# Causal mask of transposed attention scores: VectorE's minimum on the exponentials instead of identity products

## What is computed

```python
x = x + _layernorm(_L0_attn_ref(_layernorm(x), W_attn, b_attn, W_proj, b_proj))

def _L0_attn_ref(x, W_attn, b_attn, W_proj, b_proj):   # 16 heads of 16 columns
    q, k, v = split(x @ W_attn + b_attn)                # q and k then get the rotary factors
    att = einsum('bhqd,bhkd->bhqk', q, k) / sqrt(hd)
    att = where(tril, att, -inf)                        # causal
    y = einsum('bhqk,bhkd->bhqd', softmax(att), v)
    return y.reshape(B, T, C) @ W_proj + b_proj
```

## Time and profile before

| | |
|---|---|
| three runs | 3014.14, 3021.38, 3021.91 us |
| median | 3021.38 us |
| the profiled execution's own time | 3020.04 us |
| its span in the trace | 3018.3 us |
| busy share of the span | TensorE 85%, VectorE 54%, ScalarE 40%, GpSimd 30% |

### The profile page before, as it was taken

The page is one execution under the profiler, slowest core; times in us unless marked ns, Lnnn a source line. Parts: engine busy times, 40 slices in busy tenths (PEclk is TensorE's granted clock), DMA queues, the critical chain, the costliest instruction groups (busy, mean ns, idle before and its releaser), DMA issues. The chain is left out here.

```text
span 3018.3 us, 40610 instructions
## 1 busy us (share of the span) xinstructions
PE 2563.3 (85%) x14316; PEld 1528.3 (51%) x14316; DVE 1633.8 (54%) x4637; ACT 1206.3 (40%) x1994; POOL 910.8 (30%) x1442
## 2 busy tenths in 40 slices
PE   3799999999999999995158888947899999999997
PEld 2244444444545444442137777734566666656664
DVE  2667676767677675772743444342444443443443
ACT  1266666666566666564122232202322322322221
POOL 6040524426160716134012111011324233243142
PEclk9699999999999999998577887968999999999999
DMA  2442250605251524301401111121111021021010
GB/s 96 120 127 72 87 154 35 197 32 170 61 179 51 160 81 141 86 17 56 151 4 54 34 50 52 46 56 48 51 35 44 31 69 43 29 71 43 15 43 28
DMA packets 156117, 220.25 MB, mean 73 GB/s; under 512 B 18591, under 2 KB 122987, under 8 KB 149676
## 3 DMA queue, kind: packets, MB, share of 16 engines
q1 hardware_dynamic: 151820, 213.65, 23.0%
q0 software_dynamic: 4096, 4.01, 0.5%
HBM read 113.75 MB, written 103.88 MB: 72 GB/s over the span
## 5 line engine op out<-in xcount | busy, mean ns | idle before, releaser
L1009 ACT ACTIVATE pt<-ps 128x1024 f32<-128x1024 f32 (+3 forms) x768 | 599.8, 811 | 308.3 <-PE ps L924 210.3
L835 DVE CUSTOM_DVE_ANT_0 masked<-ps,mask_q 128x128 bf16<-128x128 f32 (+3 forms) x1024 | 473.4, 485 | 246.1 <-PE ps L902 243.9
L902 PE MATMUL ps<-sk,sq 96*128 96x512 bf16 (+3 forms) x1536 | 427.7, 337 | 66.5 <-DMA sk<-scratch_stacks 28.9
L921 PE MATMUL ps<-sq,sk 99*128 99x512 bf16 (+3 forms) x1536 | 398.7, 329 | 13.6 <-DMA sq<-scratch_nm_parts 11.5
L839 DVE TENSOR_REDUCE mx<-ps 128x1 f32<-128x512 f32 x512 | 351.7, 687 | 91.0 <-PE ps L902 90.5
L940 PE MATMUL ps<-pt,val 128*32 128x512 f32 (+3 forms) x3072 | 328.1, 499 | 3.5 <-ACT yt L1017 3.5
L902 PEld LDWEIGHTS ps<-sk,sq 96*128 96x128 bf16 x1536 | 132.6, 97 | 385.6 <-issue 104.1
L2086 PE MATMUL ps<-w_fc,eyb 128*128 128x256 f32 x1024 | 229.3, 381 | 14.6 <-ACT eyb L2147 7.8
L921 PEld LDWEIGHTS ps<-sq,sk 99*128 99x128 bf16 x1536 | 147.4, 98 | 161.0 <-ACT pt L1009 59.1
L2074 PE MATMUL ps<-eht,w_fc 128*128 128x512 f32 x512 | 223.2, 594 | 1.5 <-ACT eht L2137 1.4
L2086 PEld LDWEIGHTS ps<-w_fc,eyb 128*128 128x128 f32 x1024 | 191.4, 190 | 49.3 <-ACT eyb L2147 16.1
(11 more groups left out here) (329 smaller groups left out, 4295.6 us busy)
## 6 DMA issues: line engine op xcount, KB each, us to landing
scratch_stacks<-part SPq DMA_DIRECT2D x32, 768.0 KB, 3.7
sq<-scratch_stacks SPq DMA_DIRECT2D x32, 768.0 KB, 8.9
sk<-scratch_stacks SPq DMA_DIRECT2D x32, 768.0 KB, 11.4
scratch_stacks<-part SPq DMA_DIRECT2D x32, 512.0 KB, 4.6
scratch_x<-xr SPq DMA_DIRECT2D x16, 1024.0 KB, 7.7
x<-in_L_attn_x SPq DMA_DIRECT2D x8, 1024.0 KB, 14.4
scratch_stacks<-part SPq DMA_DIRECT2D x32, 256.0 KB, 4.9
xr<-in_L_attn_x SPq DMA_DIRECT2D x8, 1024.0 KB, 6.3
```

The source lines that it names most:

```text
L835: nc.vector.tensor_tensor_reduce(mem["masked"][:, slot, 0:n], ps[:, RING[slot], 0:n], mem["mask_q"][:, BANK - n:BANK], 1.0, -3e38, ALU.add ...
L902: nc.tensor.matmul(ps[:, bank, 0:n], sq[0:ROWS, h, i * P:(i + 1) * P], sk[0:ROWS, h, half * BANK:half * BANK + n], start=True, stop=True)\
L921: last = nc.tensor.matmul(ps[:, bank, 0:n], sk[0:ROWS_M, h, j * P:(j + 1) * P], sq[0:ROWS_M, h, q0:q0 + n], start=True, stop=not diag)
L1009: nc.scalar.activation(pt[:, u % 3, 2 * pair:2 * pair + 2, 0:n], ps[:, bank:bank + 2, 0:n], ACT.Exp, scale=SCALE).then_inc(e["exp_done"], 1)
```

## The change

The identity products and their tiles (`ident16`, `mask_kq`, `zeros16`) go. Instead a tile `cap` holds 3e38 where a key may be seen and 0 where not, and for each unit on the diagonal VectorE takes the minimum of the exponentials' first 128 columns and `cap`, for four heads in one instruction ("clip", 128x512 f32, two SBUF operands). In the list of steps the clip of unit t-1 stands in turn t between part 0 and part 1 of the steps beside (exp 0, part 0, exp 1, clip, part 1, av, y_out, part 2). The value products come two units behind instead of one (`AV_LAG = 2`) and wait for the clips up to their unit; "t1" moves one turn later.

```diff
+UNBOUND = 3e38
@@ setup, GpSimd
-                nc.gpsimd.affine_select(out=w["mask_kq"][:, :], in_=w["zeros16"][:, :], compare_op=ALU.is_ge,
-                                        fill=NEG, base=0, pattern=[[1, P]], channel_multiplier=-1)
+                nc.gpsimd.memset(mem["cap"][:, :], UNBOUND).then_inc(capped, 1)
+                g.wait_ge(capped, 1)
+                nc.gpsimd.affine_select(out=mem["cap"][:, :], in_=mem["cap"][:, :], compare_op=ALU.is_ge,
+                                        fill=0.0, base=0, pattern=[[1, P]], channel_multiplier=-1)
@@ setup, VectorE
-                nc.vector.memset(mem["mask_q"][:, 0:BANK - P], 0.0)
-                nc.vector.memset(w["zeros16"][:, :], 0.0).then_inc(zeroed, 1)
+                nc.vector.memset(mem["mask_q"][:, 0:BANK - P], 0.0).then_inc(zeroed, 1)
...
-                nc.vector.tensor_copy(w["ident16"][:, :], w["ident"][:, :]).then_inc(turned, 1)
@@ order of the steps
+AV_LAG = 2
+def on_diagonal(g):
+    half, j, q0, n = EU[g]
+    return q0 == j * P
+def clips_until(t):
+    whole, rest = divmod(t, len(EU))
+    return whole * sum(on_diagonal(g) for g in range(len(EU))) + sum(on_diagonal(g) for g in range(rest))
...
-            put(behind + 1 + i // 2, ("t1", b, i))
+            put(behind + 2 + i // 2, ("t1", b, i))
...
         if t < turn * B:
-            for pair in range(2):
-                order += [("exp", t // turn, *divmod(t % turn, n_eu), pair)] + cut[pair]
+            order += [("exp", t // turn, *divmod(t % turn, n_eu), 0)] + cut[0]
+            order += [("exp", t // turn, *divmod(t % turn, n_eu), 1)]
         else:
-            order += cut[0] + cut[1]
+            order += cut[0]
         if 0 < t <= turn * B:
             b, (s, g) = (t - 1) // turn, divmod((t - 1) % turn, n_eu)
+            order += [("clip", b, s, g)] if on_diagonal(g) else []
+        order += cut[1]
+        if AV_LAG <= t < turn * B + AV_LAG:
+            b, (s, g) = (t - AV_LAG) // turn, divmod((t - AV_LAG) % turn, n_eu)
             order.append(("av", b, s, g))
@@ VectorE
+                if kind == "clip":
+                    s, g = a
+                    u = turn * b + s * n_eu + g
+                    v.wait_ge(e["exp_done"], 2 * u + 2)
+                    nc.vector.tensor_tensor(pt[:, u % 3, :, 0:P], pt[:, u % 3, :, 0:P],
+                                            spread(mem["cap"][:, :], 1, HS), ALU.min).then_inc(e["clipped"], 1)
@@ TensorE, exp and av
-                        diag = q0 == j * P
                         last = nc.tensor.matmul(ps[:, bank, 0:n], sk[0:ROWS_M, h, j * P:(j + 1) * P],
-                                                sq[0:ROWS_M, h, q0:q0 + n], start=True, stop=not diag)
-                        if diag:
-                            last = nc.tensor.matmul(ps[:, bank, 0:P], w["ident16"][:, :], w["mask_kq"][:, :],
-                                                    start=False, stop=True)
+                                                sq[0:ROWS_M, h, q0:q0 + n], start=True, stop=True)
...
                     pe.wait_ge(e["exp_done"], 2 * t + 2)
+                    if on_diagonal(g):
+                        pe.wait_ge(e["clipped"], clips_until(t + 1))
```

More of the change, by code:

```diff
@@ L119, in setup_attention @@
         masked = m.sem("masked")
+        capped = m.sem("capped")
         zeroed = m.sem("zeroed")
@@ L217, in _ @@
                     nc.vector.tensor_copy(w["wqkv"][:, k, 2 * C:3 * C], wqkv_raw[:, k, 2 * C:3 * C])
-                    nc.vector.tensor_scalar(bvrep[:, k, :], ones[:, :], bv[:, k:k + 1], None, ALU.mult)
-                nc.vector.tensor_copy(w["ident16"][:, :], w["ident"][:, :]).then_inc(turned, 1)
+                    last = nc.vector.tensor_scalar(bvrep[:, k, :], ones[:, :], bv[:, k:k + 1], None, ALU.mult)
+                last.then_inc(turned, 1)
                 v.wait_ge(cols, 1)
@@ L401 @@
 TABLES = {
-    "ident": ([P, P], F32), "ident16": ([P, P], BF16), "mask_kq": ([P, P], BF16),
-    "zeros16": ([P, P], BF16), "zeros32": ([P, P], F32), "mask_f32": ([P, P], F32),
+    "ident": ([P, P], F32), "zeros32": ([P, P], F32), "mask_f32": ([P, P], F32),
     "bdmask": ([P, HC, S1], F32), "mhalf": ([P, NT], F32),
@@ L646, in attention_loop @@
             "junk": m.sb("junk", [P, NT, C], BF16),
-            "mask_q": m.sb("mask_q", [P, BANK]), "masked": m.sb("masked", [P, len(RING), BANK], BF16),
+            "mask_q": m.sb("mask_q", [P, BANK]), "cap": m.sb("cap", [P, P]), "masked": m.sb("masked", [P, len(RING), BANK], BF16),
         }
         names = """x_in x_stat head_step x_rstd x_ready
-            parts_step nm_ready nm_step nmp_ready nm_out s_full exp_done av_done yt_ready xr_in a_stat tail_step a_rstd a_norm x1_ready x1_stat x1_rstd xn1_ready
+            parts_step nm_ready nm_step nmp_ready nm_out s_full exp_done clipped av_done yt_ready xr_in a_stat tail_step a_rstd a_norm x1_ready x1_stat x1_rstd xn1_ready
             x1_stored scored keep_step kept xn2_ready x2_ready stored""".split()
@@ L829, in _ @@
                     slot, uses = bank_use(step)
-                if kind == "max":
+                if kind == "clip":
[4 more added lines that the diff above has]
+                                            spread(mem["cap"][:, :], 1, HS), ALU.min).then_inc(e["clipped"], 1)
+                elif kind == "max":
                     s, n_unit = a
```

## The result

The changed kernel takes 3077.34 us, the median of four runs (3073.4 to 3084.2), against 3018.18 before: a ratio of 1.0199 [1.0173, 1.0224], +59 us where +19 was forecast. The forecast's time was 3039 us, and the range ended at 3072: the measured time lies above it. Its profiled execution has a span of 3073.8 us; a body in the middle of the loop (mean of five) takes 170.5 us instead of 163.5.

What follows compares the result with a forecast made beforehand. VectorE's fullness was to decide in some stretches, TensorE's pace elsewhere. Terms 2.88 - 1.29 + 0.80 gave +2.4 us a body, +19 over 8 bodies on 3020.0: 3039 us; range 3003 to 3072.

Steps and rivals of the forecast that it cites:

- A: Stretches into and through set 0: +1.33 us a body, from turns 10, 11 and 2, 3; turns 0, 1 shorter by 0.48.
- B: Set 1's stretches: turns 10, 11 +0.46 us, turns 0 to 3 with room -0.96, together -0.50 us a body.
- C: Set 2's stretches: turns 10, 11 +0.91 us, turns 0 to 3 -0.96, together -0.05 us a body.
- D: Set 3's stretches: turns 10, 11 +0.94 us, 0, 1 +1.09, 2 to 4 +1.51, together +3.54 us a body.
- Turn by turn: Sum over a body's stretches, each the greater of VectorE's time with clips and old length less products: +2.88 us a body.
- VectorE has 8 us of room: Set 2, where GpSimd is busy 18.88 of 20.24 us: VectorE's room covers its exclusion by GpSimd, so nothing is added.
- GpSimd's 0.8: Set 3's turns 0 to 4: five clips wait for GpSimd operations that exclude VectorE, +0.8 us a body.
- Identity products: 1024 products hold 61 us of TensorE, 0.24 us a turn; time saved in turns 10 and 11 is waited away.
- Value products one unit later: Wide ones leave turns 1 and 5, lightening them where TensorE sets the pace: -1.29 us a body.
- Faster: the clips are hidden: Rival: clips fit VectorE's gaps around TensorE's score pairs; 2968 us, or 3003 if only set 3 pays; chance 0.22.
- No difference: the clip is cheap: Rival: a clip costs 0.45 us instead of 0.60, +0.1 us a body, 3021 us; chance 0.16.
- Dearer: GpSimd and VectorE shut each other out: Rival: clips in set 3 and turns 10, 11 of sets 1, 2 wait whole GpSimd operations; 3072 us; chance 0.15.

Runs made afterwards that it cites:

- clip_half: Changed kernel with clips of 64 instead of 128 columns a head, the rest of the mask left out: 3037.18 us, 1.0057 of the kernel before.
- place_by_set: Changed kernel with the clips of set 1's turns 1 to 4 and set 2's turns 2 and 3 moved to their turn's end: 3067.77 us, 1.0152.
- clip_last: Changed kernel with every clip moved to the end of its turn, behind all the maxima beside it: 3135.71 us, 1.0379 of the kernel before.
- reduce_instead: Changed kernel with each clip replaced by a maximum over the same 512 elements with one SBUF operand, mask left out: 3075.86 us, 1.0182.
- no_mask: Changed kernel without clips, and without identity products, so no causal mask on the transposed scores: 2992.66 us, 0.9914 of the kernel before.
- clip_unit8: Changed kernel with VectorE's clip for unit 8 alone and identity products for the other units: 3010.95 us, 0.9966 of the kernel before.
- lag_alone: Changed kernel's order of steps alone, with identity products kept and no clips: 3017.75 us, 0.9995 of the kernel before.
- mix_a: Changed kernel with GpSimd's select for unit 8 of all sets and units 0 to 3 except in set 2, identity products elsewhere: 3010.61 us, 0.9971.
- clip_early: Changed kernel with value products one unit behind and t1 where it was before the change: 3202.69 us, 1.0606 of the kernel before.
- both_masks: Changed kernel with identity products kept beside the clips on the diagonal: 3097.44 us, 1.0262 of the kernel before.

## Why the prediction was wrong in size

The direction was right, and so were the mechanism in the stretches where VectorE was counted as the fuller and the price of a clip in VectorE's queue. The time was 38 us short of the measured one, the change 40 us: the clips cost 86 us where 60 were forecast, the products gave 25 instead of 31, the later value products 2 instead of 10. By sets, against the forecast, a body lost 0.6 us more in A, 2.7 in B and 2.2 in C, and 0.8 less in D: the miss lies in B and C.

**The step that failed** is the rule of "Turn by turn": "A stretch's new length is the greater of its VectorE time plus 0.60 a clip, and its old length less 0.24 a masked turn", with "turns 0 to 3 have room" and the clip of turn 4 "hidden in the same way". It compares two sums of busy time over a stretch, as if work could be moved within it. VectorE works through a list, and a clip ahead of a maximum can delay that maximum, and TensorE behind it, even where VectorE idles later in the same turn. The table shows 5.3 us a body, 42 us in all, in stretches to which the rule gave 0; clip_half shows that the cost goes with the length. What lies behind it differs by set:

- B, 2.18 us: shown. place_by_set and clip_last give back 1.8 of it by moving the clips behind the maxima.
- C, 2.17 us: shown for some 0.6, the exclusion of GpSimd (reduce_instead); 0.46 of it is the clip of turn 4, whose cost clip_last leaves as it was. The prediction gave GpSimd nothing here, since "VectorE has 8 us of room": the same step. Of the rest, clip_last gives back the 0.42 of turn 3. Some 1.1 us in turn 0 stay open: that they are the clip's place is read from the list alone, and clip_last doesn't shorten that turn.
- A, turns 0 and 1, 1.08 us: not the place. The forecast took 6.10 us as the length without clips (5.67 with the later value products); the order alone made it 4.59, and so VectorE decides there too.

For turn 4 the prediction said "where that cover fails each costs up to 0.60"; it cost 0.57 in B, 0.56 in C (seen in turn 5) and nothing in A.

**The other terms of the sum:**

- Clips in the full stretches: forecast +6.7 a body and +0.8 for GpSimd in D, measured +5.9; D's clips last 0.67 to 0.74 us, so GpSimd's 0.8 isn't there. D's total agrees, +3.54 over turns 10 to 4, measured 5.72 + 6.97 + 9.24 - 5.08 - 6.05 - 7.30 = +3.50, but in part by luck: turns 10, 11, 0 and 1 cost 0.5 us less than forecast, and turns 2 to 4 cost 0.4 more, about what the clock costs there (last section). Turns 10 and 11 were dear in the forecast (+3.2 in four sets) and cost 1.95.
- All clips: forecast 60 us (7.5 x 8), measured 86: 42 us more where 0 was given, 13 us less where they were priced (1.6 x 8), by the profile's bodies.
- Identity products: 3.84 a body, 31 us; measured 3.8 a body and 25 us in the runs. Turns 4 to 9 gave 1.43 (forecast 1.44 for turns 8 and 9). That the sum agrees is luck: turns 0 to 4 gave 1.7 (forecast 2.40), and turns 10 and 11, where the saving should be "waited away", 0.65.
- Value products one unit later: -1.29 a body, measured -0.36. A gave -0.77 (forecast -0.86; turns 0 and 1 lost 2.0 us and turns 4 to 9 gained 1.1, more than the moved products hold, as "t1" moved too), B -0.31 (-0.43), but C lost 0.61 and D 0.11 where lighter and heavier turns were to cancel: turns 10 and 11 grew by 0.9 in the four sets, D's turns 2 to 4 by 0.43, and the turns that the wide products left gave little in C and D.
- The price of a clip, 0.60 us in the queue, was right (0.59 from the clip to the next maximum), as were 0 for the value products' wait (0.2 us in all). The prediction gave 0 also for VectorE's wait for the exponentials; the clips' group has 52.3 us of idle time before it, but in all bodies except the last it lies at the clip of turn 9 (1.4 us in B and C, 1.0 in D), and turn 9 is as long as without clips (3.60 us in B and C).

**The rivals.** "Faster: the clips are hidden" falls with no_mask and clip_half. It named the right gaps, "around TensorE's score pairs", but a clip uses one only if it stands in front of it; the clip of turn 9 costs nothing, and clip_unit8, which has it alone, is faster. "No difference: the clip is cheap" falls with 685 ns a clip. "Dearer: GpSimd and VectorE shut each other out" came nearest in time (3072), and its sign, clips of over 1 us, showed in 19 of the 256. But it needed 4.1 us a body more, about half of it in D; reduce_instead, which has no second SBUF operand, gives 0.6 to 1.1, and D's clips meet next to nothing. The right outcome was in none of the cases: clips that cost time in the stretches with room too.

What the section on what would show it said of B and C, "near their old length", was the sign that fell first: B grew by 1.42 us and C by 1.80 a body.

## What to carry to other kernels

An engine's idle share in a stretch doesn't say that an added instruction is hidden. In B it would have been only if the idle time lay at the instruction's place in its list, ahead of the next thing that another engine waits for; look at the timeline of one turn, not at two sums. With a shallow ring between two engines, take the full length of an instruction that stands ahead of a ring operation as its price until a run says otherwise (on average 0.44 of 0.60 us were paid in B and C). Check also whether another part of the same change empties a stretch, as it did in A. And when two whole times are equal, compare the stretches before saying that nothing changed. When work is to move from one engine to another, move the part that falls in real idle time (here one unit of twelve) and leave the rest.

## What the runs showed of the hardware

TensorE's granted clock fell inside the loop. In the kernel before it is 1.00 in every stretch of the earlier trace rows; over 130 to 1250 us of the span the lower level is granted for 3.0 us in all, and for none in lag_alone, no_mask, clip_unit8 and mix_a. In the changed kernel it is 23.9 us, 34 in reduce_instead, 69 in clip_last, 96 in clip_early. In every middle body of the changed kernel it falls in set 3's turns 2 to 4; here is the body shown, in three windows:

```profile
...
754.73:757.25 2.52, 2.30 (x16) 0.66 (x14) 2.52 (x10) 1.08 (x2) 1.07 (x3) 1.00 0.03 7
757.25:761.20 3.95, 2.91 (x19) 1.01 (x20) 3.74 (x15) 0.66 (x2) 2.06 (x4) 0.83 0.38 122
761.20:764.45 3.25, 3.25 (x18) 1.13 (x17) 2.74 (x9) 1.94 (x2) 0.00 (x0) 0.68 1.04 349
...
```

1.00 is the level of 2.4 GHz; 0.83 and 0.68 are mixtures with the level of 1.2 GHz. Ahead of the fall VectorE was busy 2.52 of 2.52 us and TensorE's score products waited for it. The same turns in both_masks, where VectorE is as full and TensorE has the identity products in the pauses:

```profile
...
761.52:770.31 8.79, 7.65 (x59) 2.92 (x58) 8.79 (x29) 3.68 (x6) 3.12 (x6) 1.00 0.45 146
...
```

8.79 us is what the forecast gave for these turns (7.30 + 1.51 = 8.81); in the body of the changed kernel shown above they take 9.72 with the clock down. But two other bodies of the changed kernel take 8.81 and 8.84 us with 3.4 us at the lower level too, so the same time at the lower level doesn't always cost the same. Other bodies of both_masks fall too (10.2 us in the loop), so the identity products alone don't prevent it. What makes the clock fall was not settled. Its price in the changed kernel, as an estimate from the mean of five bodies, is 9.24 - 8.79 = 0.4 to 0.5 us a body, some 3 to 4 us in all. In reduce_instead the same turns take 8.70 us in the one of six bodies without a fall and 10.63 to 10.87 in the three with 10.2 us at the lower level over turns 0 to 4: 2 us more.
